# Two-block transformer on one core: the scores of a token with itself made by VectorE products and summing matmuls

## The chip, the core and the metric

The kernel runs on one NeuronCore of a Trainium2 chip. The core has five engines that run side by side and meet through semaphores: TensorE (PE) for matmuls, VectorE (DVE) and ScalarE (ACT) for elementwise work, GpSimd (POOL) and SyncE (SP), which here issues DMA transfers. The metric is the device time of one launch in microseconds (us). Before the change it is 3713.05 us, the median of 3 runs (3710.95 to 3714.19).

## The reference, cut to what matters

The program is two blocks, each of an attention-like layer and a mixture of experts. The change is in the second block's first layer, a gated linear recurrence over complex numbers with 8 heads of 32 channels:

```python
u = silu(x @ W_in.T + b_in)
qkva = (u @ W_qkva.T + b_qkva).reshape(b, Ls, Hh, Dd, 4, 2)
c = complex(qkva[..., 0], qkva[..., 1])
q, k, v, a = c[..., 0], c[..., 1], c[..., 2], c[..., 3]
mag2 = a.real * a.real + a.imag * a.imag
a = a * (rsqrt(mag2) * sigmoid(log(mag2)))
kv = einsum('blhd,blhe->blhde', k, v)         # plus a * h0 at the first token
h_t = a_t * h_(t-1) + kv_t                    # associative_scan over tokens
y = einsum('blhd,blhde->blhe', q, h)
```

Everything is float32. There are 4 batches of 1024 tokens and a model width of 256.

## The kernel before

The kernel walks over 8 segments of 128 tokens, for all 4 batches at once (`NT` = 512 columns). Each segment is one turn of `turn(seg, rest, nxt, pre)`; a turn also holds work for the next segment (`nxt`, absent in the last) and for the one after it (`pre`, absent in the last two). After the segments come the 39 expert tiles of the last layer, which this change does not touch. No scheduler is at work: the order of every engine is the order in which its own block of the program is written, and an engine waits only where a `wait_ge` stands.

In the recurrence the 8 heads are split into two groups of four (`hg` = 0 and 1). The scan is written as masked scores between queries and keys, made in 8 steps: step 0 gives the score of a token with itself, steps 1 to 7 ("levels") give the scores between neighbouring blocks of 1, 2, 4, ... tokens, after VectorE has multiplied queries and keys by the running product of `a`. The order of a segment is this.

- **PE** makes 12 planes (L1850; planes 0, 1 are `a`, 2, 3 `q`, 4, 5 `k` of group 0; 6 to 11 the same of group 1). ScalarE takes each out of PSUM (L824). Then PE calls `level(hg, k)` for k = 0 to 7 and hg = 0, 1. `level` at k = 0 is 128 matmuls of 32 by 32 keys and 64 columns for each group (L2158). Between the four batches of `level(0, 0)` stand the value matmuls of one batch, `value_columns(b)` (L2111, L2113), into banks 4 to 7. The profile counts two records for each float32 matmul.
- **ScalarE** takes the magnitude's square root (`mag_sqrt`, L815), for group 1 after all planes; then the values of the four batches (L835, L837), then fills the state table for group 0 (`fill_state(0)`, L843, 8 instructions), and only then takes the blocks of level 1 (`take_blocks(1, hg)`, L910), and so on through the levels. After them come `take_outputs(0)` (L882), `fill_state(1)` (L843), `take_keys(0)` and `take_keys(1)` (L889).
- **VectorE** scales `a` for both groups (L1452 to L1459). For each group it then multiplies the queries (L1466, L1467), waits for the scores of step 0 (`scored`), adds (L1469, it overwrites the queries that step 0 reads), negates (L1470) and copies the scores under a mask into `near_score` (`take_scores(hg, 0)`, L1409). Then come the levels: for each level and group L1494 to L1511, with a wait for `scored` in front of L1508, and behind them `take_scores(hg, level)`, L1416 for the first level and L1422 for later ones, which waits for `block_ok` of ScalarE.
- **PE** after the levels: `outputs(0)` (L2178, L2183), `turn_keys` (L2196), `state_add(0)` (L2206, waits for `take_keys(0)`), `next_rows` (L1869, where `pre`), `outputs(1)` (waits for `fill_state(1)`, semaphore `hx_ok`), `state_add(1)`.
- **GpSimd** clears score tiles; those in `ring` (L1760) after the planes and values are made.

The short names in the rows are the program's tensors: `arena` is one large SBUF tensor with most tiles in it, `banks` is PSUM, `ring` holds streamed weights, `xn` holds the keys of group 1 in this stage.

Of the kernel before, what the change touches and what calls it, by code (L numbers as in the profile page):

```python
# [23 lines left out]
ALU = mybir.AluOpType  # L24
# [100 lines left out]
def build(nc, ins, out):  # L125
    with ExitStack() as ctx:
# [132 lines left out]
        def level_table(hg, lev):  # L259
            n = NT >> lev  # L260
            if lev == LEVELS:
# [14 lines left out]
                 for v in (h_tok[:, :, :].rearrange("p b d -> p (b d)"), y2_flat[:, 2 * NT:4 * NT])]  # L276
        first_raws = [score[:, :, :, :, SEG - BLK + i * BLK // 2:SEG - BLK + (i + 1) * BLK // 2] for i in range(HG)]
# [161 lines left out]

        zeroed = signal("zeroed", rest=6)  # L440
# [225 lines left out]
        def _(act):  # L666
# [11 lines left out]
            def turn(seg, rest, nxt, pre):  # L678
# [105 lines left out]
                if rest:  # L784
# [32 lines left out]
                    for hg in range(HG):  # L817
                        Q3, K2, TT = Q3s[hg], K2s[hg], TTs[hg]
                        for c in range(6):
# [9 lines left out]
                            if n == 3:  # L829
                                mag_sqrt(0)  # L830
                    mag_sqrt(1)
# [100 lines left out]
                    take_outputs(0)  # L932
                    fill_state(1)
                    take_keys(0)
# [100 lines left out]
        def _(dve):  # L1035
# [69 lines left out]
            def turn(seg, rest, nxt, pre):  # L1105
# [186 lines left out]
                if rest:  # L1292
# [108 lines left out]
                    def take_scores(hg, k):  # L1401
# [6 lines left out]
                        if k == 0:  # L1408
                            dve.copy_predicated(  # L1409
                                near_score.rearrange("p h b r t -> p h (b r) t"),  # L1410
                                near_masks[:, 0:BLK].bitcast(I32).unsqueeze(1).unsqueeze(1).to_broadcast([P, HP, 2 * B, BLK]),
                                banks_[:, 4 * hg:4 * hg + HP, 0:2 * B * BLK].rearrange("p h (g t) -> p h g t", g=2 * B))\
                                .then_inc(*up(masked, me))
# [31 lines left out]
                    for hg in range(HG):  # L1445
# [13 lines left out]
                        dve.tensor_tensor(a2, a2, twice(t1[:, 0]), ALU.mult).then_inc(*up(a_ok, me))  # L1459
                        settle()  # L1460

                    for hg in range(HG):
# [5 lines left out]
                        dve.wait_ge(*at(scored, hg + 1))  # L1468
# [152 lines left out]
                if pre:  # L1621
# [3 lines left out]
                             logit_sub, comb_ok, comb_copied, hid0_ok, x_done, mag_ok, a_ok,  # L1625
# [96 lines left out]
        def _(pool):  # L1722
# [8 lines left out]
            def turn(seg, rest, nxt, pre):  # L1731
# [17 lines left out]
                if rest:  # L1749
# [7 lines left out]
                    pool.wait_ge(*at(plane_mm, 6 * HG))  # L1757
# [37 lines left out]
        def _(pe):  # L1795
# [32 lines left out]
            def turn(seg, rest, nxt, pre):  # L1828
# [202 lines left out]
                if rest:  # L2031
# [83 lines left out]

                    def level(hg, k):
# [3 lines left out]
                        if k == 0:  # L2120
                            pe.wait_ge(*at(plane_ok, 6 * HG))
                            if hg:
                                pe.wait_ge(*at(v3_ok, B))
                        else:
                            if lev:
                                pe.wait_ge(*at(k_ready, 2 * lev + hg - 1))
                            if lev == 0:
                                pe.wait_ge(*at(masked, hg + 1))
                            elif lev <= INNER:
                                pe.wait_ge(*at(block_ok, 2 * (lev - 1) + hg + 1))  # L2130
                            else:
                                pe.wait_ge(*at(laid_middle, hg + 1))
                        pe.wait_ge(*(at(q_ready, 2 * (k - 1) + hg + 1) if k else at(q_neg, hg + 1)))
                        for b in range(B):
                            for r in range(2):
                                for x in range(HP * NCH if k == 0 else 2 * HP if lev == INNER else HP):
# [3 lines left out]
                                    if k == 0:  # L2140
                                        n = (h + x // HP) % NCH
                                        keys = slice(BLK * n, BLK * n + BLK)
                                        q = q[:, :, keys]
                                        width = 2 * BLK
                                    elif lev < INNER:
# [14 lines left out]
                            if k == 0 and hg == 0:  # L2160
                                if b == B - 1:
                                    i_.then_inc(*up(scored))
                                value_columns(b)
                        if k or hg:
                            i_.then_inc(*up(scored))
# [46 lines left out]
                    for k in range(STEPS):  # L2212
                        for hg in range(HG):
                            level(hg, k)
# [286 lines left out]
```

## Time and profile before

| what | value |
|---|---|
| median of 3 runs | 3713.05 us |
| the profiled execution | 3732.9 us |
| its span in the trace | 3730.7 us |
| PE busy | 2893.2 us (78%) |
| DVE busy | 2051.5 us (55%) |
| ACT busy | 1153.9 us (31%) |
| POOL busy | 657.4 us (18%) |
| mean granted TensorE clock | 0.833 |
| the chain that ended last, by engine | PE 56%, DVE 20%, ACT 7%, POOL 6%, issue 4% |
| L2158, all steps and both groups | 2 x 6144 matmul records, 205.6 + 188.9 us busy |

The eight segments fill about 3000 us of the span; one takes about 350 us and the recurrence's levels about 120 us of it. Shares over the whole span say little about one stage, so the stage is read from the chain of waits and from the timeline of a segment. The times in rows count from the start of the span. The recurrence of the first segment begins at about 404 us, that of the last at about 2845 us. TensorE's clock is granted at one of two levels, 2.4 GHz (shown as 1.00) and 1.2 GHz (0.50).

### The profile page before, as it was taken

How to read it: one execution, taken by the hardware profiler on the slowest of the kernel's cores; microseconds unless marked ns; L12 is line 12 of the kernel's file. 1: busy time of each engine (PE TensorE's matmuls, PEld its weight loads, DVE VectorE, ACT ScalarE, POOL GpSimd, SP SyncE). 2: the span in 40 equal slices, each digit the busy share in tenths (PEclk: the TensorE clock that was granted, in tenths of full speed). 3: DMA queues.
4: the chain of work that ended last, by engine and by line, in shares of the span. 5: the costliest groups of instructions: out<-in, count | busy, mean ns of one | idle time of the engine just before them, and what ended most of it. 6: DMA issues, size and time to landing. Idle time of an engine off the chain costs nothing.

```text
span 3730.7 us, 82066 instructions
## 1 busy us (share of the span) xinstructions
PE 2893.2 (78%) x35840; PEld 2138.0 (57%) x35840; DVE 2051.5 (55%) x4592; ACT 1153.9 (31%) x2228; POOL 657.4 (18%) x682
## 2 busy tenths in 40 slices
PE   4358769877996888698869977886789539999990
PEld 3245457445744664575457545744555538888880
DVE  4445776676668567855776676668444830000004
ACT  0212353144324422432353145324413512222210
POOL 0322400420060016003400520061001000000006
PEclk8678978887797879697978887797779769999995
DMA  2122201311031122012201210121100025556555
GB/s 82 24 57 48 51 2 48 73 30 41 25 72 15 41 47 57 8 41 58 52 2 42 69 40 11 44 72 21 41 28 31 2 85 188 196 190 197 193 162 168
DMA packets 230022, 247.56 MB, mean 66 GB/s; under 512 B 147360, under 2 KB 187168, under 8 KB 227360
## 3 DMA queue, kind: packets, MB, share of 16 engines
q1 hardware_dynamic: 223520, 225.54, 21.1%
q0 software_dynamic: 6144, 16.79, 1.4%
q8 instruction: 282, 4.62, 0.5%
q14 instruction: 76, 0.62, 0.1%
HBM read 196.15 MB, written 46.14 MB: 65 GB/s over the span
## 4 chain that ended last, share of the span: by engine, by line
PE 56%; DVE 20%; ACT 7%; POOL 6%; issue 4%; DMA 1%; SPq 0%; POOLq 0%; DVEq 0%
PE banks L1850 13%; PE banks L2366 7%; PE banks L2385 7%; POOL arena L1746 4%; PE banks L2158 3%; PE banks L2178 2%; PE banks L2183 2%; PE banks L1860 2%; DVE arena L1177 2%; PE banks L1977 2%; POOL arena L1790 2%; PE banks L2113 2%; PE banks L1982 2%; PE banks L1987 1%; PE banks L1956 1%
## 5 line engine op out<-in xcount | busy, mean ns | idle before, releaser
L1746 POOL TENSOR_TENSOR arena<-arena 128x1 f32<-128x1 f32 (+30 forms) x496 | 438.3, 914 | 585.4 <-DMA arena<-n_d 461.3
L1767 POOL DMA_INDIRECT h_d<-h_tok,pos_now x64 | 66.2, 1034 | 1578.3 <-DVE pos_now L1611 1561.2
L2158 PE MATMUL banks<-arena 32*32 32x64 f32 (+2 forms) x6144 | 205.6, 313 | 172.6 <-DVE arena L1511 102.8
L1177 DVE TENSOR_REDUCE arena<-arena 128x1 f32<-128x1 f32 (+30 forms) x496 | 243.5, 502 | 164.2 <-POOL arena L1746 159.6
L1850 PE MATMUL banks<-hT,ring 128*128 128x512 f32 x640 | 313.8, 643 | 7.7 <-DVE arena L1321 7.4
L2158 PEld LDWEIGHTS banks<-arena 32*32 32x32 f32 (+2 forms) x6144 | 184.4, 193 | 212.3 <-DVE arena L1511 117.9
L2158 PE MATMUL banks<-arena,xn 32*32 32x64 f32 (+2 forms) x6144 | 188.9, 310 | 142.5 <-DVE xn L1511 116.6
L2366 PE MATMUL banks<-arena 128*128 128x256 f32 x1248 | 276.9, 380 | 0.0
L2385 PE MATMUL banks<-arena 128*128 128x256 f32 x1248 | 275.7, 379 | 0.0
L1029 ACT ACTIVATE arena<-banks,arena 128x256 f32<-128x256 f32 x312 | 130.7, 470 | 455.9 <-PE banks L2366 455.9
L2158 PEld LDWEIGHTS banks<-arena,xn 32*32 32x32 f32 (+2 forms) x6144 | 173.8, 188 | 160.8 <-DVE xn L1511 126.1
L2366 PEld LDWEIGHTS banks<-arena 128*128 128x128 f32 x1248 | 237.9, 191 | 32.9 <-issue 0.4
L910 ACT ACTIVATE arena<-banks 32x512 f32<-32x512 f32 (+1 forms) x288 | 169.2, 588 | 270.1 <-PE banks L2158 201.9
L2385 PEld LDWEIGHTS banks<-arena 128*128 128x128 f32 x1248 | 234.2, 190 | 30.3
L1850 PEld LDWEIGHTS banks<-hT,ring 128*128 128x128 f32 x640 | 125.8, 204 | 186.7 <-issue 185.9
L1850 PE MATMUL banks<-arena,ring 128*128 128x512 f32 x512 | 224.0, 595 | 6.2 <-ACT arena L811 6.2
L1691 DVE COPY arena<-banks 128x512 f32<-128x512 f32 x39 | 27.0, 691 | 270.2 <-PE banks L2354 270.2
L1790 POOL DMA_INDIRECT arena<-y_d,y_at x64 | 64.9, 1015 | 608.4 <-DMA y_d<-arena 589.2
L1850 PEld LDWEIGHTS banks<-arena,ring 128*128 128x128 f32 x512 | 96.0, 190 | 128.4 <-issue 112.9
L1701 DVE TENSOR_TENSOR arena<-banks,arena 128x512 f32<-128x512 f32 x39 | 27.0, 692 | 249.4 <-PE banks L2385 249.4
L793 ACT ACTIVATE arena<-banks 128x512 f32<-128x512 f32 x80 | 47.8, 597 | 312.5 <-PE banks L1850 312.5
L2084 PE MATMUL banks<-ring,arena 128*128 128x256 f32 x640 | 140.5, 380 | 0.3 <-DVE arena L1321 0.3
(351 smaller groups left out, 5325.3 us busy)
## 6 DMA issues: line engine op xcount, KB each, us to landing
arena<-in_w_ring SPq DMA_DIRECT2D x78, 1024.0 KB, 5.1
ring<-in_w_ring SPq DMA_DIRECT2D x104, 512.0 KB, 4.6
arena<-h_d SPq DMA_DIRECT2D x39, 256.0 KB, 5.3
y_d<-arena SPq DMA_DIRECT2D x39, 256.0 KB, 5.8
n_d<-NA SPq DMA_DIRECT2D x8, 1024.0 KB, 3.8
arena<-n_d SPq DMA_DIRECT2D x16, 512.0 KB, 8.1
u_d<-arena SPq DMA_DIRECT2D x8, 1024.0 KB, 3.8
NA<-u_d SPq DMA_DIRECT2D x32, 256.0 KB, 6.0
```

The lines of the kernel that those rows point to most:

```text
L910: ins_ = act.activation(laid_, made, ACT.Copy)
L1029: ins_ = act.activation(hid1[:, i % 2, t], bank[pair][:, half * T1:(half + 1) * T1], ACT.Gelu, bias=b1[:, i % 2, t:t + 1])
L1177: dve.tensor_reduce(Usub[:, c, 0:t, t], part, AX.X, ALU.add).then_inc(*up(sub_sum, me))
L1746: pool.tensor_tensor(part, Usub[:, c, 0:t, 0:t], Nsub[:, c, t, 0:t].unsqueeze(1).to_broadcast([P, t, t]), ALU.mult)\
L1790: pool.indirect_dma_start(out=y_of[:, s % 3, k, b], out_offset=None, in_=y_d, in_offset=spot)\
L1850: i_ = mm(dst, w[:, k, cols_], rhs(src, k), start=(k == 0), stop=(k == n - 1))
L1860: i_ = mm(bank[banks[j]][:, i * D:(i + 1) * D], src[:, k, 2 * j + i, :], w[:, k, :], start=(k == 0), stop=(k == KC - 1))
L1977: i_ = mm(bank[6 + k][q, j * P:(j + 1) * P], WT[:, k, j, q], S0[:, k, (j - c) % B, :], start=True, stop=True)
L2084: i_ = mm(bank[DOWN_BANKS[b]][:, 0:D], hid0[:, i, b, :], downs[d][:, i - first, :], start=(i == 0), stop=(i == TILES0 - 1))
L2158: i_ = mm(bank[4 * hg + h][keys, b * width:(b + 1) * width], K2[rows_, r, b, keys], q, start=(r == 0), stop=(r == 1), skip_group_check=True)
L2366: i_ = mm(bank[t // 2][:, (t % 2) * T1:(t % 2 + 1) * T1], w1[:, i % 2, t // 4, at_:at_ + P], h_cols[:, i % 2, k], start=(k == 0), stop=(k ...
L2385: i_ = mm(bank[4 + i % 2][:, j * D:(j + 1) * D], hid1[:, i % 2, t, j * P:(j + 1) * P], w2[:, i % 2, t // 4, t % 4 * D:(t % 4 + 1) * D], st ...
```

## The change

The scores of a token with itself are no longer made by 256 small matmuls a segment. VectorE multiplies queries and keys elementwise (two products of 128 x 1024 for each group, into `ring` and `hT`, `same_token`), right behind the scaling of `a` of that group. PE then sums over the channels of each head: 16 matmuls for each group with 128 x 128 products as weights and 4 columns moving (`same_tokens(hg)`), into `bank[hg]`. `take_scores(hg, 0)` copies these sums, spread over 32 columns, and the wait for `scored` stands there and no longer in front of the addition. The value matmuls of batches 0 and 1 stand between the two groups' sums, those of batches 2 and 3 between `level(0, 1)` and `level(1, 1)`. `level(0, 1)` waits until both groups are masked, since it overwrites both banks. ScalarE takes the square root of group 1 after plane 9, and its `take_keys(0)` stands ahead of `fill_state(1)`. GpSimd's last clearing waits for both groups' sums.

```diff
+        same_token = ((ring[:, 4, :], ring[:, 0, :]), (ring[:, 1, :], hT[:, :, :, :].rearrange("p k b t -> p (k b t)")))
...
@@ ScalarE
-                            if n == 3:
-                                mag_sqrt(0)
-                    mag_sqrt(1)
+                            if c == 3:
+                                mag_sqrt(hg)
...
                     take_outputs(0)
+                    take_keys(0)
                     fill_state(1)
-                    take_keys(0)
                     take_keys(1)
@@ VectorE
                         if k == 0:
+                            dve.wait_ge(*at(scored, hg + 1))
                             dve.copy_predicated(
                                 near_score.rearrange("p h b r t -> p h (b r) t"),
                                 near_masks[:, 0:BLK].bitcast(I32).unsqueeze(1).unsqueeze(1).to_broadcast([P, HP, 2 * B, BLK]),
-                                banks_[:, 4 * hg:4 * hg + HP, 0:2 * B * BLK].rearrange("p h (g t) -> p h g t", g=2 * B))\
-                                .then_inc(*up(masked, me))
+                                bank[hg][:, 0:HP * 2 * B].rearrange("p (g h) -> p h g", h=HP).unsqueeze(3)
+                                .to_broadcast([P, HP, 2 * B, BLK])).then_inc(*up(masked, me))
...
                         dve.tensor_tensor(a2, a2, twice(t1[:, 0]), ALU.mult).then_inc(*up(a_ok, me))
+                        dve.wait_ge(*at(plane_ok, 6 * hg + 6))
+                        dve.wait_ge(*at(q_neg, hg + 1))
+                        dve.wait_ge(*at(plane_mm, 8 + 4 * hg))
+                        for r in range(2):
+                            ins_ = dve.tensor_tensor(same_token[hg][r].rearrange("p (c t) -> p c t", c=2),
+                                                     Q3[:, 1 - r:3 - r].rearrange("p c b t -> p c (b t)"),
+                                                     twice(K2s[hg][:, r].rearrange("p b t -> p (b t)")), ALU.mult)
+                        ins_.then_inc(*up(same_ok, me))
...
-                        dve.wait_ge(*at(scored, hg + 1))
                         step(dve.tensor_tensor(q2, t1[:, :, :], t2[:, :, :], ALU.add))
@@ GpSimd
-                    pool.wait_ge(*at(plane_mm, 6 * HG))
+                    pool.wait_ge(*at(scored, HG))
@@ PE
+                    def same_tokens(hg):
+                        pe.wait_ge(*at(same_ok, hg + 1))
+                        for b in range(B):
+                            for c in range(2):
+                                at_ = (2 * b + c) * HP
+                                for r in range(2):
+                                    t = slice(c * NT + b * SEG, c * NT + (b + 1) * SEG)
+                                    i_ = mm(bank[hg][:, at_:at_ + HP], same_token[hg][r][:, t], const("head_of"),
+                                            start=(r == 0), stop=(r == 1))
+                        i_.then_inc(*up(scored))
...
+                        if lev == 0:
+                            pe.wait_ge(*at(masked, HG))
...
-                    for k in range(STEPS):
+                    pe.wait_ge(*at(plane_ok, 6 * HG))
+                    same_tokens(0)
+                    value_columns(0)
+                    value_columns(1)
+                    same_tokens(1)
+                    level(0, 1)
+                    value_columns(2)
+                    value_columns(3)
+                    level(1, 1)
+                    for k in range(2, STEPS):
                         for hg in range(HG):
                             level(hg, k)
```

Line numbers after L277 move up by 1 to 13. The next two listings are PE's order in a segment between the planes and level 2, before and after. Before, L2158 with 32x64 is step 0, with 128x128 a level; L2111 and L2113 are the value matmuls.

```order
L2158 MATMUL banks<-arena 32x64 [waits q_neg,plane_ok]
L2158 MATMUL banks<-arena 32x64 x31
L2111 MATMUL banks<-rows,consts 128x512 [waits ring_in3]
L2113 MATMUL banks<-ring,arena 128x512 x2
L2158 MATMUL banks<-arena 32x64 x32
...
L2158 MATMUL banks<-arena,xn 32x64 [waits q_neg,v3_ok,plane_ok]
L2158 MATMUL banks<-arena,xn 32x64 x127
L2158 MATMUL banks<-arena 128x128 [waits q_ready,masked]
L2158 MATMUL banks<-arena 128x128 x31
L2158 MATMUL banks<-arena,xn 128x128 [waits q_ready,masked]
L2158 MATMUL banks<-arena,xn 128x128 x31
```

After, L2133 is the summing matmul, L2120 and L2122 are the value matmuls and L2171 is the level.

```order
L2133 MATMUL banks<-consts,ring 128x4 [waits same_ok,plane_ok]
L2133 MATMUL banks<-consts,ring 128x4 x15
L2120 MATMUL banks<-rows,consts 128x512 [waits ring_in3]
L2122 MATMUL banks<-ring,arena 128x512 x2
...
L2133 MATMUL banks<-consts,ring 128x4 [waits same_ok]
...
L2171 MATMUL banks<-arena 128x128 [waits q_ready,masked]
L2171 MATMUL banks<-arena 128x128 x31
L2120 MATMUL banks<-rows,consts 128x512 [waits ring_in3]
L2122 MATMUL banks<-ring,arena 128x512 x2
L2120 MATMUL banks<-rows,consts 128x512 [waits ring_in3]
L2122 MATMUL banks<-ring,arena 128x512 x2
L2171 MATMUL banks<-arena,xn 128x128 [waits q_ready,v3_ok,masked]
```

The value matmuls of two batches have moved from ahead of the mask copies to behind the first level of group 0. ScalarE's order between the planes and the first level's blocks is the same in both; this is it after the change (L836, L838 values, L844 the state table, L911 the blocks that VectorE's first masked copy of a level waits for).

```order
L836 ACTIVATE arena<-banks 128x8x64 [waits v_mm]
L838 ACTIVATE arena<-banks 128x8x32
L844 ACTIVATE arena<-H 32x4x64 [waits zeroed]
L844 ACTIVATE arena<-H 32x4x64 x7
L911 ACTIVATE arena<-banks 32x32x16 [waits scored,zeroed]
```

The pair L836, L838 stands four times, once for each batch, ahead of L844. ScalarE behind the levels, before and then after, where L882/L883 take outputs, L843/L844 fill the state table of group 1 and L889/L890 take the keys:

```order
L882 ACTIVATE arena<-banks 128x512 [waits y_mm] x2
L843 ACTIVATE arena<-H 32x4x64 x8
L889 ACTIVATE arena<-banks 128x256 [waits kt_mm]
L889 ACTIVATE arena<-banks 128x256 x3
L889 ACTIVATE xn<-banks 128x256 [waits kt_mm]
```

```order
L883 ACTIVATE arena<-banks 128x512 [waits y_mm] x2
L890 ACTIVATE arena<-banks 128x256 [waits kt_mm]
L890 ACTIVATE arena<-banks 128x256 x3
L844 ACTIVATE arena<-H 32x4x64 x8
L890 ACTIVATE xn<-banks 128x256 [waits kt_mm]
```

The four takes of group 0's keys have moved ahead of the eight fills.

## Rows read from the trace of the kernel before

**Rows 1.** Chain in order of time, segment 0: start us, us, what

```profile
426.76 1.05 PE banks L2111 x2
427.81 1.91 PE banks L2113 x4
...
446.78 1.24 DVE arena L1469
...
449.71 0.69 DVE arena L1494
```

**Rows 2.** Timeline, segment 0, DVE: start, duration, engine, line, [idle before <-releaser]

```profile
438.12 1.23 DVE L1469 TENSOR_TENSOR arena<-arena 128x1024 f32<-128x1024 f32 x1 [7.17 <-PE banks L2158]
...
446.78 1.23 DVE L1469 TENSOR_TENSOR arena<-arena 128x1024 f32<-128x1024 f32 x1 [3.26 <-PE banks L2158]
...
448.39 1.28 DVE L1409 COPY_PREDICATED arena<-near_masks,banks 128x1024 f32<-128x1024 int32 x1
...
455.84 1.30 DVE L1416 COPY_PREDICATED h_tok<-near_masks,arena 128x512 f32<-128x512 int32 x1
```

**Rows 3.** Line L1469, what it waited for: us in total, times

```profile
  PE banks L2158: 85.7, 16
```

**Rows 4.** Line L1458, what it waited for: us in total, times

```profile
  ACT arena L815: 12.9, 9
```

**Rows 5.** Timeline, segment 7, DVE's second L1452

```profile
2858.86 1.23 DVE L1452 TENSOR_TENSOR arena<-arena 128x1024 f32<-128x1024 f32 x1 [2.30 <-ACT arena L824]
```

**Rows 6.** Timeline, segment 0: ScalarE and PE up to the first level's blocks

```profile
441.01 0.60 ACT L835 ACTIVATE arena<-banks 128x512 f32<-128x512 f32 x1 [2.88 <-PE banks L2113]
441.50 0.38 ACT L837 ACTIVATE arena<-banks 128x256 f32<-128x256 f32 x1
441.77 2.94 ACT L843 ACTIVATE arena<-H 32x256 f32<-32x256 f32 x8
...
446.61 2.10 PE L2158 MATMUL banks<-arena 32*128 32x128 f32 x64
448.83 2.39 ACT L910 ACTIVATE arena<-banks 32x512 f32<-32x512 f32 x4 [4.13 <-PE banks L2158]
```

**Rows 7.** Timeline, PE: matmuls with few moving columns, at either clock

```profile
28.08 13.79 PE L1810 MATMUL banks<-silu_c,arena 128*128 128x4 f32 x64
...
109.24 1.92 PE L1924 MATMUL banks<-consts,arena 128*128 128x8 f32 x16 [0.66 <-ACT arena L720]
...
115.91 3.58 PE L1924 MATMUL banks<-consts,arena 128*128 128x8 f32 x16 [3.40 <-ACT arena L733]
```

**Rows 8.** Windows, PE: stretch, us, busy, granted clock, DMA share, GB/s

```profile
112.00:116.00 4.00, 0.60 (x4) 0.50 0.02 4
...
426.00:441.00 15.00, 14.98 (x280) 1.00 0.01 2
...
456.00:498.00 42.00, 24.90 (x448) 0.67 0.05 14
```

**Rows 9.** Timeline, segment 0, PE: the projection after a wait, then the planes

```profile
397.74 5.74 PE L1850 MATMUL banks<-hT,w_in 128*128 128x512 f32 x8 [1.45 <-ACT hT L804]
...
404.26 20.87 PE L1850 MATMUL banks<-arena,ring 128*128 128x512 f32 x48 [0.78 <-ACT arena L811]
```

**Rows 10.** Timeline, segment 0, behind the levels

```profile
533.98 1.09 PE L2196 MATMUL banks<-consts,arena 128*128 128x128 f32 x8
...
537.55 1.21 ACT L889 ACTIVATE arena<-banks 128x256 f32<-128x256 f32 x4
...
542.16 0.61 PE L2178 MATMUL banks<-arena 128*128 128x128 f32 x4
```

**Rows 11.** Line L2206, what it waited for: us in total, times

```profile
  ACT arena L889: 48.5, 16
```

**Rows 12.** Timeline, segment 7, behind the levels

```profile
2973.37 1.09 PE L2196 MATMUL banks<-consts,arena 128*128 128x128 f32 x8
...
2979.85 1.23 PE L2178 MATMUL banks<-arena 128*128 128x128 f32 x4
```

More of the change, by code:

```diff
@@ L438, in build @@
         rt_exp = signal("rt_exp", rest=1)
+        same_ok = signal("same_ok", rest=2)
         zeroed = signal("zeroed", rest=6)
@@ L1624, in turn @@
                 counted(seg, [pre_var, pre_rows, rank_read, dve_step, ln_var_ok, xn_ok, px_free, conv_ok, kp_ok, na_ok, sub_ok, sub_sum, z_ok, s_ok, o_var, on_ok,
-                             logit_sub, comb_ok, comb_copied, hid0_ok, x_done, mag_ok, a_ok,
+                             logit_sub, comb_ok, comb_copied, hid0_ok, x_done, mag_ok, a_ok, same_ok,
                              q_ready, masked, state_ok, hsq_ok, rt_var, rt_gap, hot_ok,
@@ L2119, in level @@
                         lev = k - 1
-                        if k == 0:
-                            pe.wait_ge(*at(plane_ok, 6 * HG))
+                        if lev:
+                            pe.wait_ge(*at(k_ready, 2 * lev + hg - 1))
+                        if lev == 0:
+                            pe.wait_ge(*at(masked, HG))
                             if hg:
                                 pe.wait_ge(*at(v3_ok, B))
-                        else:
[L2125 to L2133, printed above, removed]
+                        elif lev <= INNER:
+                            pe.wait_ge(*at(block_ok, 2 * (lev - 1) + hg + 1))
+                        else:
+                            pe.wait_ge(*at(laid_middle, hg + 1))
+                        pe.wait_ge(*at(q_ready, 2 * lev + hg + 1))
                         for b in range(B):
                             for r in range(2):
-                                for x in range(HP * NCH if k == 0 else 2 * HP if lev == INNER else HP):
+                                for x in range(2 * HP if lev == INNER else HP):
                                     h = x % HP
@@ L2139, in level @@
                                     q = Q3[rows_, 1 - r:3 - r, b]
[L2140 to L2145, printed above, removed]
+                                    if lev < INNER:
                                         keys = slice(0, SEG)
@@ L2159, in level @@
                                             start=(r == 0), stop=(r == 1), skip_group_check=True)
[L2160 to L2165, printed above, removed]
+                        i_.then_inc(*up(scored))
                     def outputs(hg):
```

## The prediction, made before the changed kernel had run

> **What bounds the kernel now.** I read the page's chain first, then the chain in order of time through one segment, then that segment's timeline, and last the sums by line over all eight segments.
>
> PE has the largest part of the chain and VectorE the second. In segment 0's recurrence it runs through PE (step 0 of group 0 and the value matmuls, one batch after another) and hands over to VectorE at L1469 [rows 1]. From 449.71 us, the first instruction of the levels, VectorE has work without a break for about 50 us. So the stage is paid by the date at which VectorE can walk through the levels. Before them it stands still: 7.17 us ahead of L1469 for group 0 [rows 2], and 85.7 us over the 16 times in the program [rows 3], 10.7 us a segment. That is the wait which the change takes away.
>
> Behind this there is a second date. The first masked copy of a level, L1416 at 455.84 us [rows 2], needs ScalarE's blocks. Now they are ready long before: ScalarE takes them from 448.83 for 2.39 us [rows 6], so until 451.2, a slack of 4.6 us. ScalarE's list ahead of these blocks is values of four batches, then eight fills of the state table, in that order, before the change and after it. A later value matmul makes the blocks later.
>
> **The change, part by part.** Durations are of the profiled execution, 3732.9 us (span 3730.7); it stands 19.9 us above the median of 3713.05, and I carry the difference over unchanged. I count in segment 0 and check with the sums.
>
> *VectorE up to the second mask copy.* Gone are 85.7 us of waits for step 0 [rows 3]. Gone too are the waits for the square root, 12.9 us [rows 4], since ScalarE now makes group 1's root after plane 9. The added products are not shown in the trace. A float32 product of this size, L1469, takes 1.23 us [rows 2]; the best case is that all four hide, the worst that they run apart at 1.3 each, 5.2 us a segment. I take 1.2 each (back to back, a little overlap), 4.8 a segment and 38.4 in all. In segment 7 VectorE waits 2.30 us for a plane [rows 5], and the product fills that. Sum: (85.7 + 12.9 + 2.3 - 38.4) / 8 = 7.8 us earlier a segment. In segment 0 it is 7.17 + 3.26 [rows 2] + 1.6 - 4.8 = about 7.3. The second mask copy, which ended at 449.67 (448.39 + 1.28) [rows 2], would end at about 442.2. I leave its duration at 1.28 us; the source is now 32 numbers spread out instead of 1024 read, and I see nothing near in the trace to price that: it may be 0.3 less or 0.6 more a copy (the masked copies shown take 1.28 and 1.30).
>
> *From there to the first level's blocks.* After the change a chain stands here that PE and ScalarE run: `level(0, 1)` 2.1 us [rows 6], the values of batches 2 and 3 at 1.05 + 1.91 = 2.96 each [rows 1], ScalarE's take of the last 0.9, the eight fills 2.94, the blocks 2.39 [rows 6]: 14.3 us. VectorE reaches its masked copy 6.17 us after the mask (455.84 - 449.67) and then stands still for 8.1. So 7.8 us won are paid back with 8.1: +0.3 a segment, +2.4 in all. The removal of the wait is worth nothing by itself; what is late next is the value matmuls.
>
> *The summing matmuls and the clock.* 16 matmuls are 32 records. The nearest row has the same 128 x 128 weights and 8 columns: 16 records in 1.92 us at the high clock, in 3.58 at the low one [rows 7]. So 3.8 us for each group, or 7.1. The page "TensorE: Matmul & The Clock Gate" of the Trainium skill (section "Back-to-back issue gap") puts an isolated matmul of up to 64 columns at about 25 ns, which would make 0.8 us of these 3.8; the rows show 120 ns a record with a fresh set of weights each time, and they decide. By the page's figure the 0.7 below would vanish and the sum would be 5.6 us less.
>
> Such matmuls do not hold the clock. 64 of them with 4 columns ran for 13.79 us without a gap, 215 ns each throughout, the low clock's pace [rows 7]; and behind the 8-column ones at 109.24 [rows 7] the granted clock was 0.50 [rows 8]. Before the change this stretch is at 1.00 throughout (426 to 441), while the levels, with idle PE between short bursts, have 0.67 [rows 8]. What a low start costs I take from the projection at 397.74: 8 records in 5.74 us, where the planes take 20.87 / 48 = 0.435 each, 3.5 for eight [rows 9]: 2.2 us. It may be paid twice. The planes end at 404.26 + 20.87 = 425.1 [rows 9], ScalarE has the last 0.8 later; after the first sums (425.9 to 429.7) the values of batches 0 and 1 take 5.9 + 2.2 and the second sums end at 441.6, while VectorE wants them at 440.9: 0.7 us late. After the second sums PE is idle until the mask, and `level(0, 1)` with the two value batches starts low: +2.2, all on the path. The bounds: 0 if the clock stays up, and 0.7 + 2.2 + 3.3 if the second sums run low too. I take 2.9 a segment, 23.2 in all.
>
> *ScalarE behind the levels.* PE's `state_add(0)` waited for the keys, 48.5 us in 16 waits, weight load and matmul counted apart, so about 3.0 us a segment [rows 11]. In segment 0 the transposed keys are in PSUM at 535.07 and their take, 1.21 us, ends at 536.3 and not at 538.8 (537.55 + 1.21); the fills (2.93) then end at 539.25, and `outputs(1)`, which needs them, can start there instead of 542.16 [rows 10]: 2.9 us. PE has `state_add(0)` and the transposes of `next_rows` to fill the time until then; where these run at the high clock already the gain is 2.4. Average 2.5 in the six segments with `pre`. In the last two nothing stands between: the fills end at 2974.5 + 1.2 + 2.9 = 2978.6 against a start at 2979.85 [rows 12], 1.1 us. Sum -15.0 - 2.2 = -17.2. The bounds are 0, if something else holds `outputs(1)`, and -3.0 x 8 = -24.
>
> *Hidden edits.* GpSimd's clearing of `ring` comes some 9 us later and falls where VectorE stands still; the tiles are needed only behind level 5, some 50 us on. The earlier root costs ScalarE nothing, plane 10 comes from PE after it.
>
> **Sum.** 2.4 + 23.2 - 17.2 = +8.4 us. The profiled execution would be 3741.3, the median 3713.05 + 8.4 = 3721.5 us.
>
> **The rivals.**
> *The clock stays up* (the other side). If PE's work in planes and values is enough to keep it at 1.00, the 23.2 us go: 2.4 - 17.2 = -14.8, 3698.3 us. For it: the stretch before is at 1.00 through 256 small matmuls [rows 8]. Against it: the 4-column matmuls that never raised it [rows 7]. It decides at the values of batches 0 and 1: they take 5.9 us together, or 8. The same page's section "HAM oscillation — how this bites in real kernels" says that idle gaps between bursts bring the low clock back each time, which speaks against this rival; the trace agrees in the levels, at 0.67.
> *Only the second stretch is low.* The sums come in time: +0.3 + 2.2 a segment, 20.0 - 17.2 = +2.8, 3715.9 us. It needs the clock to survive 3.8 us of sums between planes and values.
> *The second sums run low as well.* 7.1 us instead of 3.8, and VectorE waits 3.3 us more ahead of the second mask copy: 8.4 + 26.4 = +34.8, 3747.9 us. For it: once fallen, the clock stayed at 0.50 through such matmuls at 115.91 [rows 7, 8]. Against: 6 us of value matmuls stand in between, and the projection recovered in about 4.
> *The gain of the keys is lost*, for instance since `outputs(1)` finds another wait: +25.6, 3738.7 us.
>
> **How the numbers follow.** Forecast, both stretches low: 0.45. Clock stays up: 0.22. Only the second low: 0.18. Second sums low too: 0.08. Keys' gain lost: 0.07. A change of 0.2% is 7.4 us, about what can be told from none. Faster by more: nearly all of the 0.22 and a little of the third case, 0.24. Within: most of the third case and the part of the forecast below +7.4, 0.28. Slower: the rest, 0.48. The low clock lasts for more or less than the one stretch I took, 1 us a segment either way, so the forecast's own range is 3713 to 3730. Holding 8 in 10 I go from 3697 (the rival on the other side) to 3738.
>
> **What would show it.** In the changed profile: no wait at the addition (old L1469) and a wait of about 8 to 12 us at the first masked copy of a level in every segment, released by ScalarE's blocks; the second mask copy ending about 16 to 17.5 us after ScalarE has taken the last plane, some 7 us sooner than before; 32 sum records taking about 3.8 us; a granted clock below 1.00 between planes and level 1; the wait of `state_add(0)` for the keys down from 3.0 to about 0.5 us. I am wrong if the first masked copy has no wait, if the two value batches behind the sums take 5.9 us at the high clock, or if `outputs(1)` does not move.

## The result, and the profile after the change

| | median of 5 runs, us | ratio to before, 95% interval |
|---|---|---|
| before | 3713.05 (3710.63 to 3722.65) | |
| after | 3736.69 (3726.36 to 3748.57) | 1.0065 [1.0035, 1.0096] |

The change makes the kernel slower by 24 us (13 to 36). The time lies inside the range (3697 to 3738 us), near its upper end, and 15 us above the forecast. The chain that ended last is made of the same engines as before (PE 56%, DVE 20%, ACT 7%):

```profile
PE 57%; DVE 19%; ACT 8%; POOL 6%; issue 3%; DMA 1%; SPq 0%; POOLq 0%; DVEq 0%
```

The timeline of segment 0 (start us, us, engine, line, tile, idle before and what ended it) shows where VectorE's wait has gone. First VectorE:

```profile
435.00 1.23 DVE L1478 TENSOR_TENSOR arena<-arena 128x1024 f32<-128x1024 f32 x1
...
443.42 1.29 DVE L1411 COPY_PREDICATED arena<-near_masks,banks 128x1024 f32<-128x1024 int32 x1 [1.28 <-PE banks L2133]
444.74 0.69 DVE L1503 TENSOR_TENSOR arena<-arena 128x512 f32<-128x512 f32 x1
...
463.06 1.31 DVE L1418 COPY_PREDICATED h_tok<-near_masks,arena 128x512 f32<-128x512 int32 x1 [12.10 <-ACT arena L911]
```

The addition (L1478, formerly L1469) waits for nothing. The second mask copy starts at 443.42 instead of 448.39 [rows 2], although this segment's first product of `a` began 1.3 us later (411.75, before 410.44). And then the first masked copy of a level stands 12.10 us, where it had no wait before. Over all segments, us in total and times, first for the mask copies L1411, then for the masked copies of levels L1418:

```profile
  PE banks L2133: 10.9, 8
```

```profile
  ACT arena L911: 97.0, 8
```

Now PE between the sums and the level, same segment and columns (two of the value matmuls' instructions, L2120 and L2122, make one batch):

```profile
426.90 4.33 PE L2133 MATMUL banks<-consts,ring 128*128 128x4 f32 x32 [0.78 <-ACT xn L826]
431.16 2.07 PE L2120 MATMUL banks<-rows,consts 1*128 1x512 f32 x2
433.16 3.72 PE L2122 MATMUL banks<-ring,arena 128*128 128x512 f32 x4
436.81 1.12 PE L2120 MATMUL banks<-rows,consts 1*128 1x512 f32 x2
437.86 1.98 PE L2122 MATMUL banks<-ring,arena 128*128 128x512 f32 x4
...
444.76 3.80 PE L2171 MATMUL banks<-arena 32*128 32x128 f32 x64 [1.45 <-DVE arena L1411]
448.34 1.90 PE L2120 MATMUL banks<-rows,consts 1*128 1x512 f32 x2
450.17 3.75 PE L2122 MATMUL banks<-ring,arena 128*128 128x512 f32 x4
453.85 1.12 PE L2120 MATMUL banks<-rows,consts 1*128 1x512 f32 x2
454.90 1.98 PE L2122 MATMUL banks<-ring,arena 128*128 128x512 f32 x4
```

The same value batch takes 5.7 us right behind the sums and 3.0 us after that; `level(0, 1)` takes 3.80 us and not 2.10 [rows 6]. The windows (stretch, us, busy, granted clock, DMA share, GB/s) say why; before, the stretch to 441 was at 1.00 [rows 8]:

```profile
431.00:440.00 9.00, 9.00 (x18) 0.68 0.00 0
...
439.68:443.31 3.63, 3.63 (x33) 1.00 0.00 0
...
445.00:457.00 12.00, 11.88 (x76) 0.64 0.16 46
456.00:498.00 42.00, 21.75 (x423) 0.72 0.01 1
```

The second row is the second sums: behind the values of batches 0 and 1 they ran at 1.00 and took 3.63 us. The first sums took 4.33 us, since the clock fell while they ran (0.84 on average). From 456 us on, the levels are as before: 0.72 against 0.67 [rows 8]. ScalarE follows the last value batch without a gap, values, fills, blocks:

```profile
456.92 0.60 ACT L836 ACTIVATE arena<-banks 128x512 f32<-128x512 f32 x1 [2.09 <-PE banks L2122]
...
457.68 2.94 ACT L844 ACTIVATE arena<-H 32x256 f32<-32x256 f32 x8
460.64 4.79 ACT L911 ACTIVATE arena<-banks 32x512 f32<-32x512 f32 x8
```

Behind the levels the keys come first. `state_add(0)` (L2214) waited 48.5 us in all for them [rows 11], and now 8.7:

```profile
  ACT arena L890: 8.7, 16
```

```profile
540.81 1.09 PE L2204 MATMUL banks<-consts,arena 128*128 128x128 f32 x8
541.94 1.21 ACT L890 ACTIVATE arena<-banks 128x256 f32<-128x256 f32 x4 [0.41 <-PE banks L2204]
543.01 2.94 ACT L844 ACTIVATE arena<-H 32x256 f32<-32x256 f32 x8
...
546.00 0.71 PE L2186 MATMUL banks<-arena 128*128 128x128 f32 x4 [0.60 <-ACT arena L844]
```

From the transposed keys (L2204, formerly L2196) to the first `outputs(1)` matmul after the fills it is 5.2 us, and was 8.2 (542.16 - 533.98 [rows 10]).

**The two profiled executions are not alike elsewhere.** Their spans are 3730.7 and 3731.1 us, though the medians differ by 24. One wait makes up for this, in a stage that the change does not touch: VectorE's first product behind the small matmuls of the first layer (old L1942 and L1946). What it waited for, before and after:

```profile
  PE banks L1946: 77.0, 15
```

```profile
  PE banks L1955: 46.6, 12
```

In that stage PE's idle time is put down to "issue" (nothing that the profile shows). A second profile of the same changed kernel, made on another chip with a span of 3774.6 us, has 80.7 us at this line, so it does not belong to the program. The profiles of the experiments below sort by the chip: 46.8 to 51.2 us in the four of the first chip, 76.5 to 80.7 in the seven of the other two, whatever the kernel. By this wait the profile of the kernel before is of the second kind, which would also explain why it stood 19.9 us above the median; its chip is not on record. I therefore compare stages by their own dates and kernels by the ratio of their medians.

**Dates by stage.** In the next table, and below, a date is a mean over the eight segments, counted from the segment's first product of `a` (the line L1452 of before).

| | before | after |
|---|---|---|
| second mask copy ends | 39.60 | 33.24 |
| ScalarE starts to take the values of batch 3 | 30.65 | 45.48 |
| first masked copy of a level starts | 45.77 | 51.61 |
| last level's scores of group 0 are laid out | 114.53 | 119.27 |
| from there to the layer's result | 39.99 | 37.69 |

The masked copy is 5.84 us later, the end of the levels 4.74, and 2.30 come back behind them. Eight times 4.74 is 37.9 us, eight times 2.30 is 18.4; the difference, 19.5 us, agrees with the measured 24 (13 to 36).

Of the 5.84 us, 1.1 are made up within the levels, at their very end: VectorE is 5.85 us later up to the last level, where it had waited for PE ahead of the addition (L1508, in five segments) and no longer does. That is 0.7 of the 1.1, from this line of before:

```profile
  PE banks L2158: 5.4, 5
```

### The profile page after: what moved, and what is told of

The parts are those of the page before. It is cut to its first block, busy times and chain, and to the rows that moved or that the text cites. A ratio compares the mean times of both kernels' runs of the same rounds, so it can differ in the third digit from the quotient of the medians.

```text
span 3731.1 us, 74938 instructions
## 1 busy us (share of the span) xinstructions
PE 2934.9 (79%) x32256; PEld 2159.1 (58%) x32256; DVE 2088.4 (56%) x4624; ACT 1154.5 (31%) x2228; POOL 656.9 (18%) x682
## 4 chain that ended last, share of the span: by engine, by line
PE 57%; DVE 19%; ACT 8%; POOL 6%; issue 3%; DMA 1%; SPq 0%; POOLq 0%; DVEq 0%
PE banks L1859 13%; PE banks L2383 7%; PE banks L2402 7%; POOL arena L1755 4%; PE banks L2122 2%; PE banks L2186 2%; PE banks L2191 2%; PE banks L2171 2%; DVE arena L1178 2%; PE banks L1986 2%; POOL arena L1799 2%; PE banks L1869 2%; PE banks L2133 2%; PE banks L1991 2%; PE banks L1996 1%
## 5 line engine op out<-in xcount | busy, mean ns | idle before, releaser
L2171 PE MATMUL banks<-arena 32*128 32x128 f32 (+2 forms) x4096 | 183.3, 375 | 168.4 <-DVE arena L1520 86.3
L2171 PEld LDWEIGHTS banks<-arena 32*128 32x128 f32 (+2 forms) x4096 | 167.2, 246 | 180.4 <-DVE arena L1520 94.7
L2171 PE MATMUL banks<-arena,xn 32*128 32x128 f32 (+2 forms) x4096 | 155.4, 336 | 126.8 <-DVE xn L1520 117.9
L911 ACT ACTIVATE arena<-banks 32x512 f32<-32x512 f32 (+1 forms) x288 | 169.2, 588 | 193.6 <-PE banks L2171 148.5
L2171 PEld LDWEIGHTS banks<-arena,xn 32*128 32x128 f32 (+2 forms) x4096 | 143.3, 218 | 144.6 <-DVE xn L1520 129.0
```

Of the source, the lines that this page charges most:

```text
L911: ins_ = act.activation(laid_, made, ACT.Copy)
L2171: i_ = mm(bank[4 * hg + h][keys, b * width:(b + 1) * width], K2[rows_, r, b, keys], q, start=(r == 0), stop=(r == 1), skip_group_check=True)
```

## The experiments

The theory after the comparison: the moves of the value matmuls behind `level(0, 1)` and the low clock that follows the 4-column sums together cost more than the wait was worth; the keys' edit gains. The rivals: the order alone is at fault (then undoing it should bring the time below that of before), the idle time of PE brings the low clock (then work in the gaps should keep it high), or ScalarE's list is what counts. Three chips were used. The kernel before took 3709.45 us on the first (values_first, fill_first, kept_busy, keys_back), 3740.79 on the second (wide_sums, wide_both, both_moves, after_again) and 3742.73 on the third (keys_alone, wide_values, wide_fill), so only ratios are compared across them. Dates are read with one reserve: each is from a single profiled execution, and where a segment stands apart it is named.

| kernel | second mask copy ends | first masked copy of a level | ratio to before |
|---|---|---|---|
| before | 39.60 | 45.77 | 1 |
| after | 33.24 | 51.61 | 1.0065 [1.0035, 1.0096] |
| after_again | 34.29 | 52.74 | 1.0098 [1.0082, 1.0114] |
| values_first | 34.31 | 49.44 | 1.0038 [1.0027, 1.0049] |
| fill_first | 33.32 | 48.76 | 1.0019 [1.0005, 1.0033] |
| both_moves | 35.91 | 48.72 | 1.0008 [0.9997, 1.0020] |
| kept_busy | 41.06 | 56.62 | 1.0221 [1.0204, 1.0237] |
| wide_sums | 31.87 | 48.55 | 1.0001 [0.9993, 1.0010] |
| wide_fill | 31.87 | 45.37 | 0.9945 [0.9926, 0.9965] |
| wide_values | 31.88 | 41.08 | 0.9841 [0.9824, 0.9858] |
| wide_both | 31.86 | 39.32 | 0.9844 [0.9831, 0.9857] |
| keys_back | 34.35 | 53.10 | 1.0128 [1.0111, 1.0144] |
| keys_alone | 40.13 | 46.30 | 0.9937 [0.9919, 0.9955] |

**values_first**: all value matmuls ahead of `level(0, 1)`.

```diff
                     same_tokens(1)
-                    level(0, 1)
                     value_columns(2)
                     value_columns(3)
+                    level(0, 1)
                     level(1, 1)
```

> The changed kernel with the value matmuls of batches 2 and 3 ahead of level(0, 1) and not behind it; nothing else differs. Theory (the blocks' chain through late value matmuls is what the change pays): the first masked copy of a level, at 51.3 us behind the first product of a, comes at 43.7 to 46.7, 4.6 to 7.6 us sooner a segment, so about 3736.7 - 45 = 3692 us, and below the kernel before. Rival (VectorE's four products and the sums are what costs, the order of the values is hidden): the copy stays within 1 us of 51.3 and the time at 3737.

Measured 3720.70 us, 1.0038. The copy starts at 49.4 and not at 43.7 to 46.7: the order helps by 2.2 us a segment and no more. The values of batches 2 and 3, now right behind the second sums, both run at the low clock's pace (segment 0):

```profile
446.08 3.78 PE L2122 MATMUL banks<-ring,arena 128*128 128x512 f32 x4
449.79 2.07 PE L2120 MATMUL banks<-rows,consts 1*128 1x512 f32 x2
451.79 3.67 PE L2122 MATMUL banks<-ring,arena 128*128 128x512 f32 x4
```

So the order is not at fault alone.

**fill_first**: ScalarE fills the state table ahead of the value takes.

```diff
+                    act.wait_ge(*at(zeroed, 2))
+                    fill_state(0)
                     for b in range(B):
                         act.wait_ge(*at(v_mm, b + 1))
...
-                    act.wait_ge(*at(zeroed, 2))
-                    fill_state(0)
```

> The changed kernel with ScalarE's eight fills of the state table (group 0) ahead of its takes of the values; nothing else differs. Theory: the fills (2.94 us) stand in the chain between the last value and the first level's blocks, so the copy comes 2.9 us sooner a segment: 3736.7 - 23.5 = 3713 us. Rival (not ScalarE's list but PE sets the date): no change, 3737.

Measured 3717.80 us, 1.0019: the copy at 48.8, 2.85 us sooner than after and as expected, the length of the eight fills. In this order the fills are on the path and the clock is untouched by them.

**kept_busy**: six more 128 x 512 matmuls a segment stand among the sums, to fill PE; their result is not used.

```diff
-                        i_.then_inc(*up(scored))
+                            if b == B - 1:
+                                i_.then_inc(*up(scored))
+                            if (hg == 0 and b < 3) or (hg == 1 and b > 0):
+                                mm(bank[2][:, :], ident, rhs(uT, 0), start=True, stop=True)
```

> The changed kernel with six extra 128 x 512 matmuls a segment into an unused bank, three among the first sums, three in and behind the second ones (their result is not used); they cost PE 5.2 us. Theory (the few-column sums let TensorE's clock fall, and that stretches levels and values by about 4 us): the granted clock stays at 1.00 between planes and level 1, levels and values 2 and 3 take 8 and not 12.2 us, the copy comes at 48 to 49.5 and not at 51.3, 3736.7 - 20 = 3717 us. Rival (the clock falls because PE waits for the mask, or falls anyway): the added work only delays, the copy comes 1 to 3 us later, 3745 to 3760 us.

Measured 3788.94 us, 1.0221: slower by far, and not as either expectation had it. The segments differ. Windows of PE over the same stage in segments 0, 3 and 4:

```profile
427.00:455.00 28.00, 27.22 (x85) 0.63 0.00 0
1505.00:1533.00 28.00, 26.73 (x166) 1.00 0.02 3
1849.00:1878.00 29.00, 27.43 (x167) 1.00 0.01 3
```

In segments 3 and 4 the clock stayed at 1.00 through the stage, in the six others it fell (the copy starts at 54.5 to 63.7 there). Where it stayed, the mask ended at 34.2 and the copy started at 48.3: 14.1 us, and my chain of level, values, fills and blocks was 14.3. With the clock up that part of the working is right. After the change this stretch takes 18.4 us, so the low clock costs 4.3 there (4.1 against my chain). How much work between the sums would hold the clock stays open.

**keys_back**: the changed kernel with `take_keys(0)` back behind `fill_state(1)`.

```diff
                     take_outputs(0)
-                    take_keys(0)
                     fill_state(1)
+                    take_keys(0)
```

> The changed kernel with ScalarE's take_keys(0) behind fill_state(1) again, as before the change. Theory: outputs(1) starts 2.9 us later in six segments and about the same in the last two, 3736.7 + 18 = 3755 us. Rival (that order is hidden behind PE's other work): 3737.

Measured 3760.24 us, 1.0128. The wait of `state_add(0)` is back at the 48.5 us of before:

```profile
  ACT arena L890: 48.5, 16
```

From the levels' end to the layer's result it takes 40.19 us again (37.69 with the edit), 20.0 us in eight segments. The medians are 23.5 us apart; but these two kernels ran on different chips, and in two of this profile's segments the copy starts 6 us later than in the others, so this difference holds more than the keys.

**wide_sums**: each sum has 128 moving columns, every head's column repeated 32 times, and VectorE copies them unspread from two banks, in two instructions of 128 x 512 for each group (that part of the edit is not shown).

```diff
-                                at_ = (2 * b + c) * HP
+                                at_ = (2 * (b % 2) + c) * P
...
-                                    i_ = mm(bank[hg][:, at_:at_ + HP], same_token[hg][r][:, t], const("head_of"),
+                                    i_ = mm(bank[hg + b // 2 * 2][:, at_:at_ + P], same_token[hg][r][:, t],
+                                            const("head_of").unsqueeze(2).to_broadcast([P, HP, BLK]),
```

> The changed kernel with each summing matmul given 128 moving columns and not 4 (every head's sum written 32 times over, into two banks a group; the mask copy is two instructions of 128 x 512). Orders and waits are the same, PE's work in the sums is more: about 4.4 us a group where it was 3.7 at the high clock. Theory (4-column matmuls let TensorE's clock fall): the granted clock stays at 1.00 from the planes to level 1, levels and values 2 and 3 take about 8 us and not 12.2, the first masked copy of a level comes at 46 to 47 and not at 51.5, 3736.7 - 43 = 3694 us. Rival (the clock falls since PE idles ahead of the sums and the level, whatever the matmuls): the copy comes at 51 to 53, 3737 to 3750 us.

```profile
428.76 3.84 PE L2134 MATMUL banks<-consts,ring 128*128 128x128 f32 x32 [0.78 <-ACT xn L826]
...
433.58 1.98 PE L2123 MATMUL banks<-ring,arena 128*128 128x512 f32 x4
```

```profile
431.00:440.00 9.00, 9.00 (x42) 1.00 0.00 0
...
438.36:442.09 3.73, 3.73 (x33) 1.00 0.00 0
440.00:457.00 17.00, 14.11 (x93) 0.67 0.10 32
```

The first 32 records take 3.84 us. They are not to be held against the 4.33 of the narrow ones, which ran in part at the low clock. The second sums ran at 1.00 in both kernels: 3.73 us here and 3.63 with 4 columns (segment 0), so 32 times as many columns cost 0.1 us. Behind the first sums the clock is 1.00 and the value matmuls take 1.98 us instead of 3.72. The mask ends at 31.7 in seven segments and 33.2 in the last, with no wait for the sums. In `level(0, 1)` and the values behind it, after PE's idle time for the mask, the clock still falls (0.67), in part of the segments less: the copy starts at 47.3 in four of eight. The ratio is 1.0001: as the theory of the clock had it for the sums, and as its rival had it for the idle time.

**wide_both**: wide sums, values first and fills first together.

> The wide sums (128 moving columns), with the values of batches 2 and 3 ahead of level(0, 1) and the eight fills ahead of the value takes. Theory: masks end at 32, PE makes the values until 36 and the level until 38, blocks are there at about 40.5, so the copy comes at 40 to 42 where the kernel before has 45.8 and the change 51.5: about 3709 - 8 x 5 - 18 = 3651 us. Rival (the clock falls all the same): about 46 to 48, 3700 us.

Measured 3680.72 us, 0.9844, faster than both kernels; the copy starts at 39.3 and not at 40 to 42. The edits are those of the three diffs above. PE, ScalarE and VectorE in segment 0:

```profile
443.89 1.98 PE L2123 MATMUL banks<-ring,arena 128*128 128x512 f32 x4
446.85 1.99 PE L2123 MATMUL banks<-ring,arena 128*128 128x512 f32 x4
448.76 2.10 PE L2173 MATMUL banks<-arena 32*128 32x128 f32 x64
```

```profile
450.99 4.80 ACT L913 ACTIVATE arena<-banks 32x512 f32<-32x512 f32 x8 [1.25 <-PE banks L2173]
...
453.41 1.32 DVE L1419 COPY_PREDICATED h_tok<-near_masks,arena 128x512 f32<-128x512 int32 x1
```

```profile
426.00:457.00 31.00, 28.00 (x287) 1.00 0.07 19
```

No batch is at the low pace in any segment, and the first masked copy (L1419) has no wait: the chain of PE and ScalarE no longer sets it.

**both_moves**: the two moves of order without the wide sums.

> The changed kernel with both orders mended (values of batches 2 and 3 ahead of level(0, 1), fills ahead of the value takes) and the sums as they are, with 4 moving columns. Theory: the gains add, 49.4 - 2.9 = 46.5 for the copy, as VectorE also waits for the level itself until then; 3720.7 - 20 = 3700 us. Rival (the level's own wait, 7 us in front of the addition, sets the date and the fills are hidden): 3718.

Measured 3745.01 us, 1.0008 beside wide_both's 0.9844 on the same chip. The difference is 4 columns or 128 and the mask copy that goes with them, which is no faster in the wide kernel (two of 0.7 us for each group, 1.29 here). The copy was expected at 46.5: it starts at 47.0 to 49.0 in four segments, at 44.1 in one, and at 50.8 to 53.9 in the three whose second sums came late. The same stretch and the values of batches 2 and 3:

```profile
426.00:457.00 31.00, 30.22 (x129) 0.72 0.00 1
```

```profile
446.59 3.78 PE L2122 MATMUL banks<-ring,arena 128*128 128x512 f32 x4
452.31 3.69 PE L2122 MATMUL banks<-ring,arena 128*128 128x512 f32 x4
```

**after_again**: the changed kernel unaltered, on the second chip.

> The changed kernel itself on this chip, beside the others. All theories: about 1.0065 of the kernel before. The spread tells of the clock: where the second sums run low too in a segment, its copy comes at about 58 and not at 51.5, so a run moves by 6 us for each such segment.

Measured 3775.49 us, 1.0098; its interval meets that of the first comparison (1.0035 to 1.0096). In segment 3 the second sums came 6 us late (37.6 instead of 31.6 to 31.9), and in segment 7 both value batches behind `level(0, 1)` ran at the low pace. What VectorE's first-layer line waited for, told of above:

```profile
  PE banks L1955: 80.7, 15
```

**keys_alone**: the kernel before with the keys' move and nothing else (the diff of keys_back the other way round).

> The kernel before with one edit: take_keys(0) stands ahead of fill_state(1). If the gain of that edit is what the stage behind the levels showed (2.85 to 3.2 us in six segments, next to nothing in the last two, 18.4 us in all), the time falls by 18 us, ratio 0.995. Rival: the gain shows only beside the later dates of the changed kernel, or a later stage swallows it: ratio 0.998 to 1.000.

Measured 3718.62 us, 0.9937 [0.9919, 0.9955], that is -23.6 us (-30 to -17). The forecast's -17.2 and the -18.4 by stages lie inside. The wait is 8.7 us, as after the change:

```profile
  ACT arena L889: 8.7, 16
```

**wide_values**: wide sums and values first, fills left where they were.

> The changed kernel with sums of 128 moving columns and all four value batches ahead of level(0, 1), the fills still behind the value takes. If the clock is what spoiled the narrow version of this order (first masked copy at 49.4 us), it stays at 1.00 here until level(0, 1); the last value take starts near 34.8, the fills end near 38.5, the blocks near 40.9 and the masked copy starts near 41: ratio to before 0.986 to 0.989. If ScalarE's fills matter more than PE's order, the copy comes at 44 or later, ratio 0.992 or more.

```profile
454.64 1.32 DVE L1419 COPY_PREDICATED h_tok<-near_masks,arena 128x512 f32<-128x512 int32 x1 [1.68 <-ACT arena L911]
```

The copy starts at 41.08, as expected, after a wait of 1.68 us; ratio 0.9841, better than the expected 0.986. Against wide_sums the copy is 7.47 us sooner, 59.8 us in eight segments, and the ratios differ by 0.0160, 59.9 us. So with the clock up the whole gain of the new order is kept.

**wide_fill**: wide sums and fills first, values of batches 2 and 3 behind `level(0, 1)`.

> The changed kernel with sums of 128 moving columns and the fills ahead of the value takes, values of batches 2 and 3 still behind level(0, 1). The chain from the mask is level 2.1, values 5.9, take 0.9, blocks 2.4 = 11.3 us at the high clock behind a mask end of 31.9, so the masked copy at 43.2 and ratio 0.990; with the low clock in this stretch, as wide_sums had it in half of its segments, 3 to 4 us later and 0.998.

The copy starts at 44.35 in six of the eight segments, 1.1 us later than 43.2, since `level(0, 1)` (3.49 us and not 2.10) begins at the low clock while the values behind it run at 1.98 us each. 0.9945 is between the two figures expected. On top of wide_values the fills' move starts the copy 1.8 us sooner (wide_both), but 0.9844 and 0.9841 cannot be told apart, and whether it is worth anything is not settled.

## Why the prediction came out as it did

The forecast of a slower kernel came true and its mechanism was found; one term was too small.

- *The removed wait.* Right. The addition has no wait, and the mask copy would end 7.8 us sooner by my sum: 39.60 - 7.8 = 31.8. The wide kernels, where no sum is late, have 31.87. The four products of segment 0 began with two in 2.35 us, so 4.7 a segment against 4.8, and the mask copy with its spread source 1.29 us, as before.
- *What is late next.* Right: the value matmuls behind `level(0, 1)` delay ScalarE's blocks, and the chain is 14.1 us with the clock up (kept_busy) against 14.3. The wait at the first masked copy is 12.1 us a segment; I had 8.1 without the clock and 11 with it.
- *The clock.* The mechanism was right, the size not: this is the term that failed. I took 0.7 + 2.2 = 2.9 us a segment, 23.2 in all. The late second sums cost 1.4 and not 0.7 (the mask ends at 33.24, without them at 31.87), and the stretch behind it 4.1 and not 2.2 (18.4 against the chain's 14.3): 5.5. I had priced a low start by the projection, where one stretch of 2.2 us is lost. Here `level(0, 1)` loses 1.7 and the first of its value batches another 2.6 (5.65 us [1.90 + 3.75] against 3.0), since the low clock outlasts the level. By wide_sums beside after_again, same chip, 4 columns and not 128 cost 4.2 us a segment in dates and 0.0097 in the ratio, 36 us, and part of the low clock is left in wide_sums.
- *The keys.* Right: -17.2 forecast, -18.4 by stages, -23.6 (-30 to -17) alone.
- *What I left out.* The 1.1 us made up at the end of the levels: 0.7 by VectorE's wait in the last level, the rest between there and the laid scores. Two small slips besides: in segment 0 the gain is 7.2 us and not 7.3, and in the last two segments the keys' gain is 2979.85 - 2978.6 = 1.25 and not 1.1. Neither moves the sum by more than 0.3 us.
- *The sum.* Forecast 2.4 + 23.2 - 17.2 = +8.4. With the measured terms: copy 5.84 x 8 = 46.7 (forecast 25.6), less 8.8 made up in the levels, less 18.4 = +19.5; measured +24 (13 to 36). That the time lies inside the range is in part luck: on the second chip the same kernel had 1.0098, which on 3713.05 us would be 3749 and above the upper end.
- *The rivals.* The one on the other side, the clock stays up, would be 3698.3 us, 0.4% below before. After the change no segment shows it; nor does any show the second stretch alone low. With the clock kept up over the sums alone (wide_sums) the kernel is level with before, and over the whole stage with the values first it is 1.6% below. The second sums run low as well in no segment of the changed kernel's first profile and in one of its second, where they took 6.83 us at 0.50 and the mask ended 5.9 us later; I had 3.3. The keys' gain was not lost.
- *The rule on the issue gap.* At a granted clock of 1.00 the 32 sum records with 4 columns take 3.63 us, 113 ns each, and those with 128 columns 3.73 us. The Trainium skill ("TensorE: Matmul & The Clock Gate", "Back-to-back issue gap") has about 25 ns for an isolated matmul of up to 64 columns, and says itself that this leaves out the weight load. Here a new set of 128 x 128 weights comes with each record, so that figure was not the one to set against them, and the trace does not show it.

So the change is two changes. The keys' move is worth -0.6% alone. The products in place of step 0 are worth a further 1.0% (0.9841 against 0.9937, same chip) once the sums are wide and the values come first; as written they cost 1.3% (keys_back, 1.0128).

## What to carry to other kernels

When a wait is removed, walk the list of the engine that feeds the next wait and date its last item: here ScalarE's values were moved behind the very instruction that VectorE's gain led up to. Here 32 records with new weights each time took 3.63 us with 4 moving columns and 3.73 with 128 at the same clock, and the work behind them ran at half the pace or at the full one; so where the clock behind such a matmul matters, try filling its columns, if only with copies. Price a low clock by what comes behind it too, not by the first burst alone, and judge an order of instructions again once the clock has been mended: values first was worth 2.2 us a segment with narrow sums and 7.5 with wide ones.

## What the runs showed of the hardware that was not expected

- At a granted clock of 1.00 the same 32 weight sets took 3.63 us with 4 moving columns and 3.73 us with 128. The clock fell while the first narrow sums ran (4.33 us at 0.84 in segment 0), not while the wide ones did (3.84 us at 1.00). The first value batch behind the narrow ones ran at about half the pace in all 48 segments of six profiles (its four long matmuls 3.6 to 3.8 us), behind the wide ones at the full pace in all 32 segments of four (1.98 or 1.99).
- In kept_busy the same instructions ran at a granted clock of 0.63 in one segment and of 1.00 in two others. With narrow sums the second sums came about 6 us late in some segments and not in others (three of both_moves, one each of after_again, values_first and keys_back): in four of the six the second sums took 6.83 us at 0.50, in the other two the first sums 6.6 and 7.0.
- A mask copy of 128 x 1024 whose source is 32 values spread over 1024 places took 1.29 us (1.28 with the full source).
- Chips differ by 30 us in one stage of PE's small matmuls: VectorE waits there 46.8 to 51.2 us in the four profiles of the first chip and 76.5 to 80.7 in the seven of the other two, whatever the kernel. The kernel before took 3709 us on the first and 3741 and 3743 on the others, so this stage is about the whole difference. Why it is slower there is not shown. A stage that a change doesn't touch has to be checked before two spans are subtracted.
